# Packed binary convolution: the offset subtraction of an image's lower half moves from VectorE to GpSimd

## Reference, cut to what matters

```python
h = _batchnorm(x, bn1_gamma, bn1_beta)
h = binary_act(h)                      # sign(h)
sw = _weight_scale(conv_w)
bw = binary_weight(conv_w) * sw        # sign(w) times one scale per channel
h = conv3x3(h, bw, padding=1, groups=16)
h = _batchnorm(h, bn2_gamma, bn2_beta) # mean and variance over all 16 images
h = h + res
return jnp.where(h > 0, h, a * h)
```

## Time and profile before

| what | us |
|---|---|
| time before, median of 3 runs (1209.4 to 1211.41) | 1209.88 |
| the profiled execution, its own time | 1208.95 |
| span of that execution in the trace | 1207.1 |

### The profile page before, as it was taken

The page is one execution under the profiler, slowest core; times in us unless marked ns, Lnnn a source line. Parts: engine busy times, 40 slices in busy tenths (PEclk is TensorE's granted clock), DMA queues, the critical chain, the costliest instruction groups (busy, mean ns, idle before and its releaser), DMA issues. The chain is left out here.

```text
span 1207.1 us, 34845 instructions
## 1 busy us (share of the span) xinstructions
PE 1042.3 (86%) x9825; PEld 714.2 (59%) x9826; DVE 918.1 (76%) x2170; ACT 787.9 (65%) x2046; POOL 564.6 (47%) x438
## 2 busy tenths in 40 slices
PE   7957698877699999999999999289999999946698
PEld 2322354444599999999999999134344444313464
DVE  5669588787677777777787777159999999964587
ACT  6866499998277777777777777166566666603475
POOL 0024047577366433333333333547898898990000
PEclk9979899998699999999999999699999999975599
DMA  7200033222133111111111111213444544332000
GB/s 223 68 0 0 3 115 102 86 69 64 36 102 96 55 46 47 48 45 40 42 43 39 44 41 40 86 35 70 110 102 118 139 114 110 90 87 90 0 1 36
DMA packets 65069, 80.98 MB, mean 67 GB/s; under 512 B 10505, under 2 KB 51101, under 8 KB 64848
## 3 DMA queue, kind: packets, MB, share of 16 engines
q1 hardware_dynamic: 51696, 46.96, 13.6%
q0 software_dynamic: 13280, 32.73, 10.8%
HBM read 36.60 MB, written 28.88 MB: 54 GB/s over the span
## 5 line engine op out<-in xcount | busy, mean ns | idle before, releaser
L590 ACT ACTIVATE Y<-ps 128x256 f16<-128x256 f32 x584 | 223.7, 383 | 127.2 <-PE ps L544 92.9
L487 POOL DMA_INDIRECT expert_out<-Y x152 | 149.5, 984 | 272.8 <-DVE Y L656 242.1
L636 DVE SCALAR_TENSOR_TENSOR Y<-ps,Y 128x256 f16<-128x256 f32 x584 | 241.4, 422 | 44.6 <-ACT Y L590 36.5
L524 PE MATMUL ps<-Y,weights 128*128 128x128 f16 x1168 | 213.0, 221 | 6.4 <-DVE Y L636 5.8
L528 PE MATMUL ps<-Y,weights 128*128 128x128 f16 x1168 | 212.8, 220 | 0.0
L525 PE MATMUL ps<-Y,weights 128*128 128x128 f16 x1168 | 212.8, 220 | 0.0
L542 PE MATMUL ps<-weights,Y 128*128 128x128 f16 x1160 | 209.9, 219 | 0.0
L543 PE MATMUL ps<-weights,Y 128*128 128x128 f16 x1160 | 209.9, 219 | 0.0
L544 PE MATMUL ps<-weights,Y 128*128 128x128 f16 x1160 | 209.9, 219 | 0.0
L1270 POOL TENSOR_TENSOR iv_pool_sum<-iv_pool_sum,iv_pool_part 128x1024 f32<-128x1024 f32 x80 | 194.0, 2425 | 7.3 <-DVE iv_pool_part L1495 0.7
L1137 POOL DMA_INDIRECT dispatched<-d_rows,slot x128 | 128.4, 1003 | 90.7 <-issue 49.5
(11 more groups left out here) (330 smaller groups left out, 2221.8 us busy)
## 6 DMA issues: line engine op xcount, KB each, us to landing
Y<-dispatched SPq DMA_DIRECT2D x152, 65.5 KB
X<-x SPq DMA_DIRECT2D x16, 512.0 KB, 4.5
iv_got<-expert_out SPq DMA_DIRECT2D x16, 512.0 KB, 4.1
out<-X SPq DMA_DIRECT2D x16, 512.0 KB, 3.0
X<-iv_pool_sum POOLq DMA_DIRECT2D x15, 512.0 KB, 4.5
X<-iv_own_sum POOLq DMA_DIRECT2D x15, 512.0 KB, 4.5
Y<-w_moe SPq DMA_DIRECT2D x8, 512.0 KB
expert_out<-Y POOLq DMA_INDIRECT x152, 2.2
```

What stands on the lines that cost most here:

```text
L487: pool.indirect_dma_start(env.yt, bass.IndirectOffsetOnAxis(ap=token[:, k:k + 1], axis=0), result[:, k, :], None, bounds_check=TOKENS - 1, ...
L524: pe.matmul(out, high, xh, start=True, stop=False)
L590: act.activation(hh[e][:, part_cols[h]], hidden[e][h], ACT.Relu).then_inc(hi_ready[e], 1)
L636: dve.scalar_tensor_tensor(hl[e][:, cols], hidden[e][h], 0.0, hh[e][:, cols], ALU.max, ALU.subtract).then_inc(h_split[e], 1)
```

## The change

The offset subtraction (*bottom*) leaves DVE's program and goes into POOL's, in which it stands behind the addition for the image two further on. POOL's program for the 16 images is written out in place of a loop of two images a turn. Nothing else is edited. Semaphores and their counts keep their meaning: `upper_ready` and `split_ready` now gate and announce the subtraction on POOL.

```diff
             def unpack(n, q, first):
-                dve.wait_ge(upper_ready, n + 1)
-                dve.tensor_scalar(bottom(n), upper[q][:, :], -CENTER, None, ALU.add).then_inc(split_ready, 1)
                 if not first:
                     dve.wait_ge(lower_ready, n + 2)
                     moments(n - 1, 0)
...
-            with by_two(pool, 0, IMAGES) as n:
-                for q in range(2):
-                    pool.wait_ge(raised, n + q + 1)
-                    pool.wait_ge(conv_ready, n + q + 1)
-                    pool.tensor_tensor(packed[q][:, :, :], high[q][:, :, :], padded[q][:, 0:PACKED, :], ALU.add).then_inc(packed_ready, 1)
+
+            def pack(n, q):
+                pool.wait_ge(raised, n + 1)
+                pool.wait_ge(conv_ready, n + 1)
+                pool.tensor_tensor(packed[q][:, :, :], high[q][:, :, :], padded[q][:, 0:PACKED, :], ALU.add).then_inc(packed_ready, 1)
+
+            def take_bottom(n, q):
+                pool.wait_ge(upper_ready, n + 1)
+                pool.tensor_scalar(CONV[:, n * PIX + HALF:(n + 1) * PIX], upper[q][:, :], -CENTER, None, ALU.add).then_inc(split_ready, 1)
+
+            for q in range(2):
+                pack(q, q)
+            for n in range(IMAGES):
+                if n < IMAGES - 2:
+                    pack(n + 2, n % 2)
+                take_bottom(n, n % 2)
```

## The result

The changed kernel takes 1234.25 us (median of 4 runs, 1232.49 to 1236.24) against 1209.64 before (4 runs; the forecast started from the 1209.88 of three of them): a ratio of 1.0207 (95% interval 1.0185 to 1.0228), slower by 24.6 us. The forecast was slower by 12.4 us, 1222.3 (1217 to 1231). The direction was right, the size half of the measured one and the range too low.

A forecast was written before the change was run, and what follows sets the result against it. DVE, full and partly waiting for POOL, was taken to set the pace. A closed DVE-POOL round gave 0.67 (start) + 10.3 (rounds) + 1.45 (end) = 12.4 us on 1208.95, so 1221.4, or 1222.3 as median; range 1217 to 1231.

The forecast's parts named there:

- What bounds the kernel now: Convolution loop: DVE is full, busy 5.66 of 5.80 us a turn, about 1.15 of each turn spent waiting for POOL.
- The closed round: Each image's round must go from DVE through POOL and back before the next begins: 3.76 us against 2.90, +10.3 for twelve.
- the even raises: Sign in the new trace: starts of raise (L306) 3.7 to 3.8 us apart and even, with no pairs.
- a PE at clock 1.00: Sign in the new trace: PE idle some 1.6 us before each product, yet at clock 1.00.
- I take 0.61: Price of POOL's subtraction on 512 elements, taken from POOL's cast because both have one input: 0.61 us.
- from above: Upper bound on the subtraction's price, from POOL's two-input addition: 1.12 us for 512 elements.
- X: Time of one POOL subtraction on 512 elements, absent from the trace: 0.61 us taken, bounds 0.52 and 1.12.
- the start: Stage up to the first top: take_bottom(0) on POOL makes top(0) start later, +0.67 us.
- the end: From raise(15) to the aggregate: 8.93 us in place of 7.48, +1.45.
- A dear subtraction: Rival: POOL's subtraction is nearer the two-input addition than the cast, 0.8 to 1.12 us, 1225 to 1230 us; 20 in 100.
- PE falls to the lower clock: Rival: PE, busy only 57%, drops to half clock, products at most 4.32 us, a round 4.4, total 1231 us; 7 in 100.
- Faster, by the end of the blocking: Rival: raise(n+3) and its addition run ahead of top(n); buffer loop of 5.2 us replaces 5.80, total 1206 us; 4 in 100.

The follow-up runs named there:

- e4_swap: The kernel before, with DVE's subtraction for image n moved ahead of raise(n+2): 1206.67 us (0.9967).
- e2_first: The changed kernel with POOL's subtraction for image n put ahead of the addition for image n+2: 1211.65 us (1.0007).
- e6_probe: The kernel before, with twelve extra POOL operations on scratch memory in the first stage, pricing the subtraction by itself: 1211.53 us, single run.
- e7_two: The changed kernel with the subtraction written as times 1.0, then minus 1536, in one instruction: 1221.5 us (1.0077).
- e8_both: The changed kernel with the subtraction as times 1.0, minus 1536 in one instruction, and ahead of the addition for image n+2: 1204.82 us (0.9946).
- e9_forms: The kernel before, with ten extra POOL operations on scratch memory in the first stage, in other forms and sizes: 1209.76 us, single run.

## Why the prediction was right in direction and wrong in size

**What bounds the kernel now: right.** DVE did wait for POOL: e4_swap took the blocking away with DVE's order alone, and the stage fell by 3.16 us. What bounds the kernel without the blocking lies close under it, a loop over one buffer of 5.20 us a turn in place of 5.80.

**The closed round: right, in place and in its parts.** In the changed kernel the steps follow each other as listed. Of the signs that the forecast gave, the even raises, DVE's wait ahead of top and POOL's wait for raise (1.78 us) came; the price of 0.61 and a PE at clock 1.00 did not. e2_first opened the round with one swap and left a stage of +4.74 where it had been +26.58.

**The step that failed: "I take 0.61", with 1.12 "from above".** The price of the subtraction was taken from the cast, because it too has one input, and the upper bound from the addition, as though a second input were the dearest thing that could be added. POOL's sum with a constant costs 2.5 ns an element (e6_probe), more than the two-input addition (2.19). The subtraction took 1.49 us, above even the upper bound. With X = 1.49, 0.88 more than taken, the working gives 0.67 + 0.88 for the start (+1.55; measured +1.45), 3.76 + 0.88 = 4.64 for a round (4.67), and 1.45 + 2 x 0.88 = 3.21 for the end (3.85). The sum is 1.55 + 12 x 1.74 + 3.21 = 25.6, and 26.58 was measured. In e7_two, where the price is what was taken, the stage rose by 12.82 against 12.4. The same sum fits both runs with this one term exchanged.

**Which of the two causes is how large.** The four kernels with either order and either price, as change of the stage against before:

| | subtraction 1.49 us | subtraction 0.62 us |
|---|---|---|
| behind the addition | +26.58 (the change) | +12.82 (e7_two) |
| ahead of the addition | +4.74 (e2_first) | -3.10 (e8_both) |

The two causes aggravate each other: in the closed round the price is paid once for each image (13.8 us between the columns), in the open one a turn of two images grows by 0.85 us from e8_both to e2_first (5.22 to 6.07), about one price for two images (7.8 between the columns). The order costs 21.8 us at the dear price and 15.9 at the cheap one. So the order, which the forecast named, is the larger cause, and the price doubled the loss (12.82 to 26.58).

On the price, the Trainium skill ("GPSIMD Engine Reference", section 3.1) gives 1.03 cycles an element for small bodies. At its 1.2 GHz the 0.83 ns an element by which the pair grows from 256 to 1024 elements in e9_forms is 1.0 cycle and agrees; the single operation's 2.5 ns is 3.0 cycles and doesn't. The measurement decides.

**The rivals.** "A dear subtraction" was the right name, but its 0.8 to 1.12 us and 1225 to 1230 us were too low, for they ended at the addition's price. "PE falls to the lower clock" came in part, and was nearly free: products took up to 3.76 us instead of 2.16, hidden inside rounds that stayed at 4.68 or 4.69. Only the last is on the path to the end, at 2.87 us (granted clock 0.74 from 147.97 to 159.30), so 0.71 us of the end's 3.85; that closes most of the gap left above. "Faster, by the end of the blocking" came to the right 5.2 us a turn, in part by luck: its sum had top (0.66) where the loop of e8_both has take_upper (0.69). And it was not two raises ahead of a top that opened the round there, but POOL's order.

**What stays open.** Why one operation costs three times as much an element as the pair on POOL isn't shown by any run, nor what two sums cost with DVE at rest. The medians of e2_first and before lie 1.3 us apart and the stages 4.74. Of the 3.4 us between, 2.7 come from the choice of executions: the profiled one of before lies 1.4 us under the median beside e2_first, the profiled one of e2_first 1.4 over its own. The stage of e2_first starts 1.75 us later, and what follows its aggregate is 2.4 us shorter; whether the shorter rest is more than the spread of single executions isn't shown.

## To carry to other kernels

Before work goes to another engine's queue, write down for one round which instruction stands ahead of it there and what that one waits for: here the moved step stood behind an addition that waited for the very engine that was to be relieved, and two lines in the other order were worth 16 to 22 us. An operation that the trace doesn't hold has no upper bound from another kind of operation; measure it alone in a stage in which its engine is idle, in each form in which it can be written. Before work is moved to end a blocking between two engines, try the order on one of them: here that was enough, with no move at all.

## Hardware behaviour that I had not expected

- POOL on 512 elements with a constant: 1.49 us for a sum, product, difference or maximum alone; 0.62 for product and sum in one instruction; 2.11 for two sums (in part beside DVE's two-input products).
- In the changed kernel PE sits idle 2.4 to 2.5 us before half of the products from 91 us on, and 0.9 to 1.8 before the others. The granted clock of four rounds in a row was 0.99, 0.65, 1.00 and 0.58 at the same work, with products of up to 3.76 us in place of 2.16, so in part at the lower of the two levels (1.2 and 2.4 GHz). In e7_two, with 1.66 us idle before nearly each, all from 90.74 us on took 2.16, and the clock of the twelve rounds was 1.00.
